# Cross-attention layer on one core: bias rows of the first two heads made during the norm, two of GpSimd's value-weight splits moved

## What is computed

```python
def _cross_attention(q_in, kv_in, wq, bq, wk, bk, wv, bv, wo, bo, bias_k, bias_v):
    qh = (q_in @ wq + bq).reshape(b, q_len, H, K)
    kh = (kv_in @ wk + bk).reshape(b, t, H, K)
    vh = (kv_in @ wv + bv).reshape(b, t, H, K)
    kh = jnp.concatenate([kh, jnp.broadcast_to(bias_k, (b, 1, H, K))], axis=1)
    vh = jnp.concatenate([vh, jnp.broadcast_to(bias_v, (b, 1, H, K))], axis=1)
    logits = jnp.einsum('bqhk,bthk->bhqt', qh, kh) / scale
    weights = jax.nn.softmax(logits, axis=-1)
    ctx = jnp.einsum('bhqt,bthk->bqhk', weights, vh).reshape(b, q_len, H * K)
    return ctx @ wo + bo

x = res + _cross_attention(_layer_norm(x, ...), xf_1, ...)
x = x + _cross_attention(_layer_norm(x, ...), xf_2, ...)
x = x + gelu(_layer_norm(x, ...) @ w_fc1 + b_fc1) @ w_fc2 + b_fc2
```

## Time and profile before

| | |
|---|---|
| median of 3 runs | 4141.71 us (4141.17 to 4147.1) |
| the profiled execution | 4142.23 us |
| its span in the trace | 4140.5 us |
| third layer in the trace | about 1593 to 4010 us |
| TensorE matmuls busy | 3851.3 us (93% of the span) |
| VectorE busy | 2905.7 us (70%) |
| ScalarE busy | 2046.3 us (49%) |
| GpSimd busy | 1744.6 us (42%) |
| mean granted TensorE clock | 0.973 |
| scaling of a score block (line 3011, `c_pr`), mean of 512 | 0.393 us |
| TensorE's wait for the exponential in head 15 of t = 7, where no value piece is split | 0.67 us |

### The profile page before, as it was taken

One profiled execution on the slowest core, in us unless ns is written; L12 is line 12 of the kernel. 1 busy time (PEld: TensorE's weight loads), 2 busy tenths in 40 slices (PEclk: granted clock), 3 DMA queues, 4 the chain that ended last, 5 costly groups with the idle time before them and its releaser, 6 DMA issues. The chain is left out here.

```text
span 4140.5 us, 68127 instructions
## 1 busy us (share of the span) xinstructions
PE 3851.3 (93%) x20348; PEld 2904.4 (70%) x20348; DVE 2905.7 (70%) x6396; ACT 2046.3 (49%) x4088; POOL 1744.6 (42%) x1216
## 2 busy tenths in 40 slices
PE   6999995789999977999999999999999999999989
PEld 3333333456666655888977988877978877978867
DVE  6667663788888864757767758757757767767755
ACT  4666662244444423555543555534555534555523
POOL 1343433678878841232244232244232344333232
PEclk8999997889999988999999999999999999999999
DMA  5444423000000002222223222123222222232223
GB/s 159 139 123 137 120 77 129 11 6 16 16 16 16 11 16 95 63 67 78 62 74 107 60 82 68 57 74 111 62 82 63 59 77 90 62 93 63 57 79 105
DMA packets 158028, 298.58 MB, mean 72 GB/s; under 512 B 18836, under 2 KB 39700, under 8 KB 156704
## 3 DMA queue, kind: packets, MB, share of 16 engines
q1 hardware_dynamic: 155752, 291.06, 22.9%
q0 software_dynamic: 1008, 3.67, 0.2%
q10 hardware_dynamic: 1032, 0.97, 0.1%
HBM read 254.21 MB, written 42.21 MB: 72 GB/s over the span
## 5 line engine op out<-in xcount | busy, mean ns | idle before, releaser
L2297 POOL TENSOR_TENSOR c_wl<-c_wr,c_wh 128x512 fp32r<-128x512 f32 (+1 forms) x576 | 821.5, 1438 | 1599.3 <-ACT c_wh L2677 1360.0
L2778 ACT ACTIVATE c_pr<-c_ps,c_nms 128x257 f32<-128x257 f32 x512 | 244.5, 478 | 472.4 <-DVE c_nms L3017 470.4
L1830 DVE TENSOR_TENSOR_SCAN b_sb<-b_wt,b_s,b_ps 128x256 f32<-128x256 f32 x512 | 356.7, 732 | 25.3 <-PE b_ps L1197 23.0
L843 DVE TENSOR_REDUCE a_nm<-a_ps 128x2 f32<-128x1024 f32 x256 | 311.9, 1222 | 74.0 <-PE a_ps L490 73.3
L2677 ACT ACTIVATE c_wh<-c_wr 128x512 fp32r<-128x512 f32 (+1 forms) x464 | 315.5, 688 | 44.5 <-PE c_ps L2384 40.7
L686 ACT ACTIVATE a_ex<-a_ps 128x1024 f32<-128x1024 f32 x256 | 260.8, 1022 | 151.6 <-PE a_ps L510 149.4
L2382 PE MATMUL c_ps<-c_hh,c_wh 128*128 128x512 f32 x768 | 307.7, 401 | 7.3 <-DVE c_hl L2883 7.3
L2382 PE MATMUL c_ps<-c_gh,c_wh 128*128 128x512 f32 x768 | 308.0, 401 | 5.2 <-DVE c_gl L3060 2.7
L1763 POOL TENSOR_TENSOR b_sb<-b_sb,b_rt 128x1024 f32<-128x1024 f32 x128 | 277.8, 2184 | 65.7 <-DVE b_sb L1830 63.8
L2384 PE MATMUL c_ps<-c_hh,c_wl 128*128 128x512 f32 x768 | 304.6, 397 | 0.0
L2383 PE MATMUL c_ps<-c_hl,c_wh 128*128 128x512 f32 x768 | 304.1, 396 | 0.0
(11 more groups left out here) (430 smaller groups left out, 10114.4 us busy)
## 6 DMA issues: line engine op xcount, KB each, us to landing
c_wr<-in_downs SPq DMA_DIRECT2D x192, 256.0 KB, 2.7
c_wr<-in_wv SPq DMA_DIRECT2D x64, 512.0 KB, 4.1
c_wr<-in_wk SPq DMA_DIRECT2D x128, 256.0 KB, 3.0
c_wr<-in_wq SPq DMA_DIRECT2D x128, 256.0 KB, 2.7
a_qp<-strips SPq DMA_DIRECT2D x64, 256.0 KB, 4.4
a_kp<-strips SPq DMA_DIRECT2D x64, 256.0 KB, 4.5
c_wr<-in_fc SPq DMA_DIRECT2D x64, 256.0 KB, 2.9
strips<-a_qh SPq DMA_DIRECT2D x32, 256.0 KB
```

What stands on the lines that cost most here:

```text
L843: dve.tensor_reduce(NM[:, s, :].rearrange("p (h c) -> p h c", h=HG)[:, 2 * p:2 * p + 2, c:c + 1], ps[:, bank:bank + 2, :], AX.X, ALU.max, ...
L1830: mm = dve.tensor_tensor_scan(SB[:, quad % RING, pr % 2, e, 1:L + 1], WT[:, third(b, i), e, :], half(spread_bank(pair), e), S0[:, b, 2 * i ...
L2297: pool.tensor_tensor(piece(WL, slot), piece(WR, slot), piece(WH, slot), ALU.subtract).then_inc(piece_cut[slot], 1)
L2778: act.activation(PR[:, i, 0:L + 1], ps[:, BS + 1 - i % 2, 0:L + 1], ACT.Exp, bias=NMS[:, i:i + 1], scale=float(K2) ** -0.5, accum_out=RS[: ...
```

## The change

- VectorE: the bias rows of heads 0 and 1 leave the place behind the key and query splits of `first_heads`. Ahead of t = 0 and odd t they are made in the norm: the first ahead of `inverse`, the second between `norm_scaled` and the last two value splits. Ahead of t = 2, 4, 6 they are made in `first_heads`, ahead of the key split.
- VectorE: for t = 0 and odd t the key split of head 1 leaves `first_heads` for head 0, between its second and third score block.
- GpSimd: the value piece `VS` of head 0 is split in head 1, between its two other pieces, behind a wait for `pb_ready` of that head. The value piece `VS + 1` of head 14, which the next attention needs, is split behind the down pieces of `j == 1`.

The number of instructions is the same on every engine. TensorE, ScalarE and SyncE keep their order.

```diff
@@ GpSimd, head() and what follows the heads
                         if at == 0:
                             pool.wait_ge(bd_ready, t * H2 + 1 + AHEAD)
                             pool.sem_inc(passed, 1)
+                        else:
+                            pool.wait_ge(pb_ready, t * H2 + 2 + AHEAD)
+                            pool.sem_inc(passed, 1)
+                            cut(VS, v_count(t, 1))
                         cut(2 * u, qk_count(t, 1))
...
-                    if u == 0 and (t + 1 < B or at < H2 - 4):
+                    if u == 0 and (at is None or 0 < at < H2 - 4):
                         cut(VS + v, v_count(t, h4 + 1))

                 head_steps(t, pool, head)
                 for j in range(1, H2 // 4):
                     for u in range(4):
                         cut(u, qk_count(t, H2 // 2 + j))
+                    if j == 1 and t + 1 < B:
+                        cut(VS + 1, v_count(t + 1, 0))
@@ VectorE, first_heads(), gap(), ahead of t = 0, head()
+            def first_rows(t, u):
+                rows(t * H2 + u, t * (H2 // 2), u)
+                dve.drain()
+
             def first_heads(t):
+                if not late_value(t):
+                    first_rows(t, 0)
+                    first_rows(t, 1)
                 keys(t * H2, 0)
                 queries(t * H2, 0)
-                for u in range(2):
-                    rows(t * H2 + u, t * (H2 // 2), u)
-                    dve.drain()
-                if late_value(t):
-                    keys(t * H2 + 1, 1)
...
                 first_values(t, 0)
+                if n % 3 == 1:
+                    first_rows(t, 0)
                 inverse(n, slice(0, N2))
                 norm_scaled(n)
+                if n % 3 == 1:
+                    first_rows(t, 1)
                 first_values(t, 1)
                 first_values(t, 2)
...
             first_values(0, 0)
+            first_rows(0, 0)
             inverse(0, slice(0, N2))
             norm_scaled(0)
+            first_rows(0, 1)
             first_values(0, 1)
...
                             if at == 1:
                                 keys(N + 1, 2)
+                            elif at == 0 and late_value(t):
+                                keys(N + 1, 1)
```

## The result

| | before | changed |
|---|---|---|
| median of 6 runs each, same chip | 4144.12 us (4141.16 to 4147.61) | 4164.75 us (4160.92 to 4166.48) |
| ratio, 95% interval | | 1.0051 (1.0038 to 1.0063) |
| profiled execution, span | 4142.23, 4140.5 us | 4163.09, 4161.4 us |
| mean granted TensorE clock | 0.973 | 0.974 |

The change makes the kernel 20.6 us slower. The forecast was 13.8 slower with a range of +3.3 to +20.3 around the median then known: the sign is right, the size is too small, and the time lies just outside the range. Against the lower group the change costs some 23 us.

What follows compares the result with a forecast made beforehand. The prediction took TensorE, busy for 93% of the span, as the bound. Its terms, 6.4 + 2.4 + 4.2 + 1.8 − 3.3 + 2.3 = +13.8 us, gave 4155.5 us against 4141.7, range 4145 to 4162.

Steps and rivals of the forecast that it cites:

- whatever delays TensorE anywhere else adds in full: Outside the looped heads of t = 1, no later stretch has TensorE slack to give a delay back.
- rows at odd t: Norm at t = 1, 3, 5, 7: two bias rows lengthen TensorE's key-split wait by 1.6 us each, +6.4 us.
- rows at t = 0: Norm at t = 0: first row starts the reciprocal 2.4 us later, 1.45 comes back, second adds 1.48; +2.4 us.
- head 1's key split in head 0: Head 0 at t = 0 and odd t: its column waits for GpSimd's split, 5 × 0.85 = +4.2 us.
- rows at even t: Ahead of t = 2, 4, 6: head 0 starts 1.75 us later, part given back; 3 × 0.6 = +1.8 us.
- the value split leaves head 14: Heads 14 and 15: 1.54 us of exponential wait and 1.8 us of scaling waits come back, −3.3 us.
- behind down piece 7: Down pieces: the moved value split delays context splits, 0.65 us at t = 1, 3, 5, 0.1 at even t; +2.3 us.
- The column loses its race: Head 0: GpSimd's slot 1 split starts before head 1's bias column, +4.2 us; rival, column first: 0, chance 0.2.
- The exponential's wait in head 15 of t = 4: TensorE's 2.21 us wait there beside a context split should become 0.67, as at t = 7; 1.54 us back.
- That small instructions don't stand still: Rival: bias rows of 12 partitions pass beside GpSimd at full speed; sum +7.7 us, 4149.4, chance 0.25 with mixtures.
- That VectorE has room in the norm: Rival: the second row costs nothing and the first heads' waits of 9.7 us go; 4128.7 us, chance 0.05.
- The pile-up in the down pieces: Rival: the next splits queue behind the value split too, 1.6 us at each odd t; 4158.4 us, chance 0.1.

Runs made afterwards that it cites:

- the lower group: Three of the six runs of the kernel before, from 4141.16 to 4141.71 us; the other three lie from 4146.53 to 4147.61.
- the undone second row: Changed kernel with the second bias row put back behind the query split at t = 0 and odd t: 4150.43 us, +8.7 against the kernel before.
- 2.8 (key split): Changed kernel with head 1's key split put back behind the query split at t = 0 and odd t: 4159.53 us, +17.8.
- 0.7 or 2.4 (even rows): Bias rows of t = 2, 4, 6: put back behind the query split in the changed kernel, 4161.68 us; moved alone on the kernel before, 4143.76 us.
- −0.75 (GpSimd): Kernel before with GpSimd's two value-split moves alone: 4140.98 us, ratio 0.9998.

## Why the prediction was wrong

**The step that failed** stands in the prediction's first part: "whatever delays TensorE anywhere else adds in full". Each delay was priced at its own length, and the clock of the matmuls behind it was put at nothing, with no reason given. The second row was charged "its 1.48 us to TensorE's wait: 1.6 with the first, 4 × 1.6 = +6.4 us". The waits did grow by that, 6.4 us over the four odd t. But behind some of the longer waits (in the changed kernel's trace at t = 0, 1, 2, 4 and 6) the matmuls ran at the lower clock level, and the undone second row gave back 11.9 us where 7.7 were waits. The trace of before had shown it behind the wait of 6.63 us at the end of t = 7 (busy time by stretch, kernel before; the clock is 0.53), and behind the 2.21 us of the earlier trace rows too, and I read neither:

```profile
3974.45:3979.00 4.55, 4.55 (x11) 3.31 (x12) 3.26 (x5) 1.44 (x2) 0.00 (x0) 0.53 0.01 4
```

In the changed kernel's trace TensorE is busy for 8.5 us more with the same matmuls, on top of 15.0 us of waits. The waits alone would have left the time inside the range. With the idle time filled the change costs 14.4 us, and with it open 20.6.

**The terms**, forecast against the waits in the trace:

| term | forecast | measured waits |
|---|---|---|
| rows at odd t | +6.4 | +6.4 (2.06, 2.39, 2.42, 2.05 for 4 × 0.63) |
| rows at t = 0 | +2.4 | +2.3 (0.96 to 2.40, and a new 0.82 for the norm) |
| head 1's key split in head 0 | +4.2 | +3.3 (4 × 0.58, 0.97) |
| rows at even t | +1.8 | +2.8 |
| the value split leaves head 14 | −3.3 | −3.3 |
| behind down piece 7 | +2.3 | +4.4 (3 × 1.19, 4 × 0.21) |
| low clock | not there | no wait, but 8.5 us of busy time; filling gave back 6.2 us of the kernel's time |

The measured waits of the table come to +15.9, the whole trace has +15.0. Two terms are mis-sized. At even t the first wait grew by 1.24 (t = 2, 4) and 1.6 (t = 6) where I had 1.75. Of the 1.34 us before head 1 I took back 0.8, and only 0.14 came. In the down pieces I gave one wait of 0.65 (2100.65 less 2098.78 less 1.3 gives 0.57). It was 0.81, the next splits do queue behind it (a second wait of 0.38), and the even t lose 0.21, not 0.1 each. A third agrees in part by luck: the odd t were forecast at 1.6 each, and measured 1.43 at t = 1 and 7 and 1.76 and 1.79 at t = 3 and 5.

**What was right.** The second row extends TensorE's wait by about its own length (1.43 us for 1.48 at t = 1 and 7), and the first is all but free at odd t. The column loses its race (1.18 us) and costs head 0 nearly what the forecast says: 0.58 for 0.85, and 0.97 at t = 7. The exponential's wait in head 15 of t = 4 falls from 2.21 to 0.67, and the scalings there go.

**The rivals.** That small instructions don't stand still is false: 1.16 to 1.24 us for a row's instructions that last 0.21 to 0.34. The Trainium skill ("SBUF — State Buffer", Who interferes with whom) has it that a VectorE instruction with two SBUF inputs and a GpSimd instruction that reads SBUF block each other, with no exception for small ones; the trace agrees, down to four elements in a partition. That VectorE has room in the norm is false as well. The pile-up in the down pieces is half true, with 1.19 us at an odd t where I gave the rival 1.6.

**Left open.** The parts come to 11.9 (second row), 2.8 (key split), 0.7 or 2.4 (even rows) and −0.75 (GpSimd): 14.7 to 16.4 of 20.6 us. The rest of 4 to 6 us is no more than the intervals leave open. Since each part's low clock depends on the others, the parts need not add up either, but that this is the whole rest was not shown. The first row's share at t = 0 and 3 (waits of 0.84 and 0.33) was not run by itself. Why one wait of 2 us and more has low clock behind it and the next has not stays open too.

## What to carry over

A wait that grows on a busy TensorE can cost more than it lasts: read the granted clock behind each wait of the profile, not its length alone, and try a few unread matmuls in it before moving other engines' work. Between two engines that block each other, an instruction's size says nothing about its price; what it meets does, and an edit that shifts one engine changes what it meets everywhere. Work that is early can be moved into a stage for nothing only up to the engine's idle time there: the first row was nearly free, the second cost some 12 us.

## What the hardware showed that I had not expected

- The granted clock fell to 0.50 behind waits of about 2 us, in a third layer that had TensorE busy otherwise, and in 29 of 39 places and not in all. Where it fell, the fall came between 0.9 us ahead of the wait's end and 1.5 us behind it: at t = 1 the window from 1891.5 to 1892.0 has 0.89, and the next 0.50.
- Extra casts of 0.2 us, 16 in a kernel of 68,000 instructions, cost 16.6 us: the waits are up by 11.5, of which only 5.4 are the waits that they stand before, and TensorE's busy time is up by 6.1.
